# Attention scores and row maxima as float32r products in 64 rows, two side by side, and dense products cut into row halves

## The reference, cut to what matters

```python
x = x + 0.5 * ffn(layernorm(x))        # r * (relu(xk @ W_k.T)**2 @ W_v.T), r = sigmoid(xr @ W_r.T)
x = x + attention(layernorm(x))        # 16 heads of 16, rotary positions, causal softmax, projection
x = x + 0.5 * ffn(layernorm(x))
# attention:
qkv = x @ W_qkv + b_qkv
att = einsum('bhqd,bhkd->bhqk', rope(q), rope(k)) / sqrt(16)
att = where(causal, att, -1e9); att = softmax(att, axis=-1)
y = einsum('bhqk,bhkd->bhqd', att, v)
```

## Time and profile before

| | us |
|---|---|
| median of 3 runs (3110.26 to 3119.8) | 3111.19 |
| the profiled execution | 3112.07 |
| its span on the core | 3110.3 |

### The profile page before, as it was taken

One profiled execution on the slowest core, in us unless ns is written; L12 is line 12 of the kernel. 1 busy time (PEld: TensorE's weight loads), 2 busy tenths in 40 slices (PEclk: granted clock), 3 DMA queues, 4 the chain that ended last, 5 costly groups with the idle time before them and its releaser, 6 DMA issues.

```text
span 3110.3 us, 56224 instructions
## 1 busy us (share of the span) xinstructions
PE 2962.3 (95%) x18245; PEld 1665.9 (54%) x18245; DVE 2475.0 (80%) x7302; ACT 2159.2 (69%) x4802; POOL 1566.6 (50%) x2190
## 2 busy tenths in 40 slices
PE   6899999999999999999999999999999999999997
PEld 4444555555555555555555555555555555555444
DVE  3888888888888888888888887888888888887872
ACT  4477777777777777777777777777767777777664
POOL 5455555555455455555555455454555555454323
PEclk9899999999999999999999999999999999999999
DMA  3443343343434352342443333343442532433421
GB/s 99 79 84 65 64 100 66 83 90 72 86 77 88 69 97 67 76 99 60 91 87 68 88 77 84 80 85 76 79 93 59 98 81 67 93 76 71 83 60 39
DMA packets 202585, 245.49 MB, mean 79 GB/s; under 512 B 68405, under 2 KB 104245, under 8 KB 202293
## 3 DMA queue, kind: packets, MB, share of 16 engines
q1 hardware_dynamic: 202293, 241.90, 37.5%
HBM read 53.48 MB, written 51.38 MB: 34 GB/s over the span
## 4 chain that ended last, share of the span: by engine, by line
PE 66%; DVE 12%; ACT 8%; POOL 6%; issue 6%; DMA 1%; SPq 1%; POOLq 0%; DVEq 0%; ACTq 0%
PE ps_y L735 14%; PE ps_s L704 12%; PE ps_m L714 11%; PE ps_d L794 7%; PE ps_d L788 6%; PE ps_d L791 5%; PE ps_d L800 5%; ACT pt_sb L830 4%; DVE ps_m L943 3%; PE ps_d L781 3%; PE ps_d L742 2%; DVE mx_sb L946 2%; PE ps_d L804 2%; POOL pt_sb L1075 2%; DVE dif_sb L974 2%
## 5 line engine op out<-in xcount | busy, mean ns | idle before, releaser
L830 ACT ACTIVATE pt_sb<-ps_s 128x512 f32<-128x512 f32 (+1 forms) x3039 | 1451.6, 495 | 816.9 <-PE ps_s L704 806.7
L943 DVE CUSTOM_DVE_ANT_0 ps_m<-ps_m,mask_sb 128x128 f32<-128x128 f32 (+3 forms) x2048 | 990.3, 498 | 370.7 <-PE ps_m L714 355.9
L704 PE MATMUL ps_s<-qr_sb,kr_sb 99*128 99x512 bf16 (+1 forms) x3039 | 994.5, 329 | 50.4 <-ACT pt_sb L830 39.3
L714 PE MATMUL ps_m<-kr_sb,qr_sb 96*128 96x512 bf16 (+3 forms) x3072 | 1000.1, 329 | 37.9 <-DVE mx_sb L943 27.7
L946 DVE TENSOR_REDUCE mx_sb<-ps_m 128x1 f32<-128x512 f32 x1024 | 697.9, 682 | 105.7 <-PE ps_m L714 97.3
L1075 POOL TENSOR_SCALAR_AFFINE_SELECT pt_sb<-pt_sb 128x512 f32<-128x512 f32 x512 | 331.4, 647 | 833.8 <-ACT pt_sb L830 833.3
L735 PE MATMUL ps_y<-pt_sb,v_sb 128*32 128x512 f32 (+3 forms) x6144 | 589.9, 494 | 3.6 <-POOL pt_sb L1075 2.7
L704 PEld LDWEIGHTS ps_s<-qr_sb,kr_sb 99*128 99x128 bf16 x3039 | 291.8, 96 | 510.0 <-issue 229.7
L714 PEld LDWEIGHTS ps_m<-kr_sb,qr_sb 96*128 96x128 bf16 x3072 | 302.0, 98 | 319.2 <-DVE mx_sb L943 71.1
L800 PE MATMUL ps_d<-axn_sb,wqk_sb 128*128 128x256 f32 x1024 | 305.3, 396 | 3.9 <-ACT axn_sb L872 3.9
L735 PEld LDWEIGHTS ps_y<-pt_sb,v_sb 128*32 128x32 f32 x6144 | 154.6, 109 | 285.9 <-issue 258.3
(11 more groups left out here) (96 smaller groups left out, 3465.5 us busy)
## 6 DMA issues: line engine op xcount, KB each, us to landing
kr_sb<-part_sb SPq DMA_DIRECT2D x378, 128.0 KB, 4.4
qr_sb<-part_sb SPq DMA_DIRECT2D x378, 128.0 KB, 4.7
y_way<-yt_sb SPq DMA_DIRECT2D x128, 256.0 KB, 2.7
sw_sb<-qb_sb SPq DMA_DIRECT2D x496, 64.0 KB, 2.0
x_sb<-x SPq DMA_DIRECT2D x64, 256.0 KB, 2.8
yn_sb<-y_way SPq DMA_DIRECT2D x64, 256.0 KB
den_sb<-r_way SPq DMA_DIRECT2D x64, 256.0 KB
out<-x_sb SPq DMA_DIRECT2D x64, 256.0 KB, 2.2
```

The source lines that it names most:

```text
L704: eng.matmul(score_bank(slot)[:, 0:width], kr_sb[0:KR + NP, n % RS, j, kb * P:(kb + 1) * P], qr_sb[0:KR + NP, n % RS, j, q0:q0 + width], s ...
L714: eng.matmul(ps_m[:, u % NM, 0:width], qr_sb[0:KR, n % RS, j, i * P:(i + 1) * P], kr_sb[0:KR, n % RS, j, piece * QC:piece * QC + width], s ...
L830: eng.activation(pt_sb[:, buffer, j, column:column + width], score_bank(slot)[:, 0:width], ACT.Exp, scale=SCALE).then_inc(exped, 1)
L943: eng.tensor_tensor_reduce(ps_m[:, u % NM, 0:width], ps_m[:, u % NM, 0:width], mask_sb[:, m0:m0 + width], 1.0, -3e38, ALU.add, ALU.max, be ...
```

## The change

1. q and k are split into two float32r parts (`r_hi`, `r_low`) instead of three bfloat16 ones. Three products of parts (48 rows) give a score, and two rows more (50) the maximum. `r_mid` and `r_rest` go.
2. Heads 0 and 2 have their rows in partitions 0 to 49, heads 1 and 3 in 64 to 113. Score j of a slot and the maximum of head `j ^ 1` therefore stand in different row halves of the array. `BESIDE` puts a maximum of the same width beside each score. Products narrower than 256 columns are computed 256 wide (`max(CH, width)`).
3. Every dense product in the steady part is cut into two halves of 64 rows, "lane" 0 and 1, that add into the same bank. Lane 1 of a product starts when its lane 0 is complete (`half_made`), beside lane 0 of the next product. Transposes are cut in the same way, lane 0 ahead of the slot's score, lane 1 behind its maximum. `ps_d` has three banks, `ps_m` two. Outside the steady part products stay whole.
4. The causal mask of the maxima is a further product into the last 128 columns (`later_sb`, `pairs_sb`, bfloat16, 64 rows), so that DVE's part is a plain reduction in all cases.
5. The rotation works in the places of the parts; `r_b0` (ACT) now waits for the rows of the batch before, where `r_hi` did. Row copies are `rows0` to `rows2` with four DMAs each, of 128 KB as before. `m_fin` has three instructions, where it had five.

```diff
-TERMS_Q = (0, 0, 0, 1, 1, 2)
-TERMS_K = (0, 1, 2, 0, 1, 0)
+TERMS_Q = (0, 0, 1)
+TERMS_K = (0, 1, 0)
-NP = 3
+NP = 2
+HALF = P // 2
-NS, NM, ND = 2, 3, 2
+NS, NM, ND = 2, 2, 3
-MAX_ORDER = [i for k in range(TT // 2) for i in (TT - 1 - k, k)]
-LEAD = 13
+BESIDE = [(3, 0), (2, 0), (1, 0), (0, 0), (4, 0), (5, 0), (6, 0), (7, 0), (7, 1), (6, 1), (5, 1), (4, 1)]
+LEAD = 17
+NU = GSLOTS
+UNITS = [(*BESIDE[m // G][:1], m % G ^ 1, BESIDE[m // G][1]) for m in ((u - LEAD) % GSLOTS for u in range(NU))]
...
-                    s("ACT", "r_mid", i, 0.53, t, ("r_rest", i, 3))
-                    s("POOL", "r_low", i, 1.2, t, ("r_mid", i, 2))
+                    s("ACT", "r_hi", i, 0.53, t, ("r_add", i, 3))
+                    s("POOL", "r_low", i, 1.2, t, ("r_hi", i, 2))
...
+        done = 0
+        for lane in (1, 0):
+            if self.lanes[lane]:
+                key, u = self.lanes[lane]
+                units = self.steps[key][1]
+                if u < units:
+                    mine.append((*key, u, lane))
+                self.lanes[lane] = key, u + 1
+                if lane == 1 and u + 1 == units:
+                    self.lanes[1] = None
...
+                if lane == 0 and u + 1 >= units and self.lanes[1] is None:
+                    self.lanes = [None, (key, 0)]
...
-        qr_sb = sb("qr_sb", [P, RS, G, T], BF16)
-        kr_sb = sb("kr_sb", [P, RS, G, T], BF16)
+        qr_sb = sb("qr_sb", [P, RS, G // 2, T], F32R)
+        kr_sb = sb("kr_sb", [P, RS, G // 2, T], F32R)
...
-                eng.matmul(score_bank(slot)[:, 0:width], kr_sb[0:KR + NP, n % RS, j, kb * P:(kb + 1) * P],
-                           qr_sb[0:KR + NP, n % RS, j, q0:q0 + width], start=True, stop=True).then_inc(scored, 1)
+                rows, more = slice(HALF * (j % 2), HALF * (j % 2) + KR + NP), max(0, CH - width)
+                eng.matmul(score_bank(slot)[:, 0:width + more], kr_sb[rows, n % RS, j // 2, kb * P:(kb + 1) * P],
+                           qr_sb[rows, n % RS, j // 2, q0 - more:q0 + width], start=True, stop=True).then_inc(scored, 1)
...
                 pe.wait_ge(max_taken, u - NM + 1)
...
+                rows, wide = slice(HALF * (j % 2), HALF * (j % 2) + KR), max(CH, width)
+                product = eng.matmul(ps_m[:, u % NM, 0:wide], qr_sb[rows, n % RS, j // 2, i * P:(i + 1) * P],
+                                     kr_sb[rows, n % RS, j // 2, piece * QC:piece * QC + wide], start=True, stop=not diagonal)
+                if diagonal:
+                    half = slice(HALF * (j % 2), HALF * (j % 2) + HALF)
+                    pe.wait_ge(masks_in, 32)
+                    product = eng.matmul(ps_m[:, u % NM, width - P:width], later_sb[half, :], pairs_sb[half, :], start=False, stop=True)
...
+                if u == 0 and lane == 1:
+                    pe.wait_ge(half_made[d], plan.split[name, i])
...
+                if u == units - 1:
+                    mm.then_inc(half_made[d] if lane == 0 else made[d], 1)
...
-                if diagonal:
-                    eng.tensor_tensor_reduce(ps_m[:, u % NM, 0:width], ps_m[:, u % NM, 0:width], mask_sb[:, m0:m0 + width],
-                                             1.0, -3e38, ALU.add, ALU.max, best).then_inc(max_taken, 1)
-                else:
-                    eng.tensor_reduce(best, ps_m[:, u % NM, 0:width], mybir.AxisListType.X, ALU.max).then_inc(max_taken, 1)
+                eng.tensor_reduce(mx_sb[:, n % 2, piece, m:m + 1], ps_m[:, u % NM, 0:width], mybir.AxisListType.X,
+                                  ALU.max).then_inc(max_taken, 1)
```

More of the change, by code:

```diff
@@ L10 @@
 BF16 = mybir.dt.bfloat16
+F32R = mybir.dt.float32r
 ALU = mybir.AluOpType
@@ L254, in apart, with free_banks, hold, divide @@
         return math.ceil(lag * 0.5) if slot < HALF_MAX else lag
+    def free_banks(self, slot):
+        return [d for d in range(ND) if self.held[d] is None or self.slots.get(self.held[d], slot) < slot - 1]
+    def hold(self, key, d):
+        self.held[d] = self.READER[key[0]], key[1]
+        self.bank[key], self.nth[key] = d, self.uses[d]
+        self.uses[d] += 1
+    def divide(self, key):
+        d = self.bank[key]
+        self.splits[d] += 1
+        self.split[key] = self.splits[d]
@@ new lines, in pick @@
+    def pick(self, e, chains, slot, xt):
+        best = None
+        for name, line in chains.get(e, {}).items():
+            if not line or name[1:] == "_T":
+                continue
+            _, cost, rank, early, after = self.steps[name, line[-1]]
+            if early > slot or not self.ready(slot, after):
+                continue
+            if name[2:] == "x0" and xt is not None and self.slots.get(self.T_OF(xt), slot) >= slot:
+                continue
+            if e == "PE" and not self.can_make(name, line[-1], slot):
+                continue
+            if best is None or (rank, line[-1]) < best[0]:
+                best = (rank, line[-1]), name, line
+        return best and (best[1], best[2].pop())
@@ L325, in place @@
-                    key = name, line.pop()
-                    if name[2:] == "x0":
+                    if e == "PE":
+                        cost, done = self.place_pe(chains, slot, mine)
+                        if not cost:
+                            break
+                        credit[e] -= cost
+                        todo -= done
+                        continue
+                    key = self.pick(e, chains, slot, xt)
+                    if key is None:
+                        break
@@ L753, in dense @@
+                start, stop = u == 0 and not lane, False
                 if name == "f_T":
                     pe.wait_ge(f_xt, CT * (i + 1))
-                    transposes(ps, xt_sb).then_inc(made[d], 1)
-                    return
-                if name == "a_T":
+                    mm, units = transposes(ps, xt_sb, k), 1
+                elif name == "a_T":
                     pe.wait_ge(a_xt, CT * (i + 1))
-                    transposes(ps, xt_sb).then_inc(made[d], 1)
-                    return
@@ L810, in _ @@
                     pv([n_ticks - NTK + k for k in BURSTS[-1]])
+                turns = plan.at["PE"].get(slot, ())
+                for name, i, u, lane in turns:
+                    if name[1:] == "_T" and lane == 0:
+                        dense(name, i, u, lane)
                 if slot in SCORE_AT:
@@ L814, in _ @@
                     maximum(u)
-                for name, i, u in plan.at["PE"].get(slot, ()):
-                    dense(name, i, u)
+                for name, i, u, lane in turns:
+                    if name[1:] != "_T" or lane != 0:
+                        dense(name, i, u, lane)
                 if slot in PV_SLOT:
```

426 lines of the change are left out of this document (198 added, 228 removed).

## The result

| | before | after |
|---|---|---|
| median of 4 runs | 3113.94 us | **3424.11 us** |
| lowest to highest | 3110.26 to 3119.8 | 3415.62 to 3431.03 |
| profiled execution | 3112.07 | 3415.62 |
| a group in the steady part, 700 to 2700 us | 46.85 | 50.58 |
| first four, last four groups | 210, 152 | 266, 186 |

The ratio is 1.099, 95% interval [1.0955, 1.1031]: 10% slower, where 2.6% faster was forecast and 3240 was the upper end of the range. Of some 300 us, 205 fall in groups 5 to 60 (2819 us against 2614; groups are counted from the first score, and their times are differences between starts of scores), 90 in the four groups at either end.

The account below looks back on a forecast made before the run. PE, busy 95% of the span, was taken as the bound; per group 40.9 + 2.35 + 2.0 + 0.4 = 45.65 us, 1.2 under 46.85, so -77 us over 64 groups: 3034 us, range 2880 to 3240.

Parts of the forecast that it names:

- PE's own work and other waits: On PE, per group of 48 slots: 40.9 us of work after the change plus 2.35 us of remaining waits.
- ring of the maxima: PE waiting for DVE's reductions with ps_m at two banks instead of three: +2.0 us a group, between 0 and 3.3.
- ring of the scores: Two score banks, with less slack for exponentials as PE's slot gets shorter: +0.4 us a group, between 0 and 0.8.
- the one on the clock: In the steady part the granted clock is 1.00, so nothing is to be had there; no term in the sum.
- over 90%: Sign of the rings taking all: DVE over 90% busy, with PE's wait for it the largest.
- the rings take it all: Rival at the score and maxima banks: 3.3 us given back and growing PE stalls, 47.3 a group, 3110 to 3140; chance 0.20.
- -3.6: PE's own work in one group of 48 slots falls from 44.5 to 40.9 us, 3.6 less.
- score and maximum together: Sign of being right, on PE: score and maximum start within 0.02 us of each other.
- 0.65 to 0.7 in wide slots: Sign of being right, on PE: a wide slot with dense work takes 0.65 to 0.7 us where nothing waits.
- PE's wait for DVE over 100 us: Sign of being right: PE's wait for DVE at the maxima goes from 28 us to over 100.
- the group: Sign of being right: a group in the steady part takes 45 to 46 us.
- halves not independent: Rival on PE: row halves keep strict pass order, 4.05 us more a group, 3370; chance 0.23, shared with loads sharing one path.

Follow-up runs that it names:

- e4: The changed kernel with VectorE's reductions over the maxima reading only the first 32 columns: 3219.87 us, ratio 1.034 to the kernel before.
- e6: The changed kernel with 32-column reductions of the maxima and, from the third group on, 32-column exponentials: 3045.96 us, ratio 0.978 to the kernel before.
- e3: The kernel before with two banks for the maxima instead of three, nothing else changed: 3276.97 us, ratio 1.052.
- m2: A products-only kernel repeating the kernel's patterns with and without waits for a VectorE copy: clock 0.54 for a lone dense product in one half with a wait.
- m3: A products-only kernel without waits, slots in halves or whole rows, with and without masks and bursts: a burst costs 1.63 us in halves, 1.53 in whole rows.
- e11: The changed kernel with score and maximum products made twice in the first and last batches (last: only slots with under two dense passes): 3428.24 us, ratio 1.101.

## Why the prediction was wrong

The sum said 45.65 a group; 50.58 was measured. By its own steps, from e4 and e6, with 0.37 to 0.5 us for each us at half clock:

| step | predicted | measured | how |
|---|---|---|---|
| PE's own work and other waits | 40.9 + 2.35 = 43.25 | 44.5 to 44.6 | e6's 44.97 less its clock |
| ring of the maxima | +2.0 (0 to 3.3) | +2.6 | after less e4 (2.77), less 0.1 to 0.2 of clock |
| ring of the scores | +0.4 (0 to 0.8) | +1.1 to 1.6 | e4 less e6 (2.84), less 1.3 to 1.7 of clock |
| clock | 0, not in the sum | +1.8 to 2.4 | 188 of the 2000 us at half clock |
| sum | 45.65 | 50.6 | |

**The step that failed first is the one on the clock**: "The granted clock is 1.00, so nothing is to be had there." That was read as a fact of the kernel, and it was a property of a queue that seldom waits: a bank less loses it in whole rows (e3), and after loses more of it, until both readers are out of the way (e6). That cost 1.8 to 2.4, the two rings' errors together 1.3 to 1.8 and PE's own work 1.3. Each of the three is as large as the 1.2 that I had forecast as the gain. The clock alone does not explain the result: without its part a group would still have taken 48.2 to 48.8, more than the 46.85 before. The Trainium skill (TensorE: Matmul & The Clock Gate, A second HAM failure mode: psum-queue depth-cycling) describes a kernel whose clock swings because TensorE pauses briefly and often while it cycles through PSUM banks; the trace after agrees in so far as its clock falls where PE has just paused (0.32 and 0.34 us in the rows above), and m2 adds that pauses alone need not do it. By that rule taking a bank away, which makes PE pause more often, was a rival with a price of its own. I had read the page for its order of matmuls only.

**The rings** were the right mechanism, mis-sized. +2.0 was measured as 2.6, inside its bounds, +0.4 as 1.1 or more, outside them. DVE was at 69%, not "over 90%" as I wanted it for a rival: a ring of two waits for an engine that has a third of its time free, since DVE's other work comes between two reductions. The rival "the rings take it all" had the right sign and less than a tenth of the size, 3110 to 3140, because it priced no clock, took 43.25 for all else and stopped both halves for nothing.

**PE's own work**: -3.6 became -2.3 at most, since e6 also has shorter other waits. The side by side slots are nearly as I computed (0.67 against 0.65); short by some 1.3 are terms at the joints. m3's patterns give 0.1 for each of seven bursts, 0.066 for each of 32 masks ((1.45 - 1.32) / 2 by the starts of two slots) where I had 0.055, and 0.66 for a wide slot where I had 0.65: together 0.7 + 0.3 + 0.4 a group, an estimate. How much of it occurs in the kernel was not measured.

**The ends** (90 us more in eight groups): the sum was for a steady group and was taken times 64, these eight included. They had 176 us at half clock against 20, worth 58 to 78 us. Whether the clock or waits for first loads lengthen them stays open; e11 could not tell.

Of the signs that I named: score and maximum together, yes; 0.65 to 0.7 in wide slots, yes; PE's wait for DVE over 100 us, yes with the load's row, 71.5 in the product's; the group, no. And the rival with the nearest number, halves not independent, was wrong in its mechanism.

## What to carry to other kernels

Ask of every change that makes TensorE's work shorter between waits, or uses part of its rows: what holds the clock up afterwards? Two queues of work in one engine's order share each wait; splitting the array does not split the queue, so a ring needs more slack after such a change, not less. And before a bank is moved from one ring to another, run the old kernel without that bank: e3, one changed digit, would have shown half of this result (163 of 310 us).

## What was not expected of the hardware

- Row halves are nearly free of each other: 1.92 times for float32r, 0.109 a dense pass against 0.217, and a later product of one half can start ahead of an earlier one of the other (1705.02 and 1705.13).
- A change between 64-row and 128-row products costs about 0.2 us each way (1.05 against 0.66 a pair).
- The same waits leave the clock at 1.00 with dense products in both halves and take it to 0.54 with one in one half alone.
- A burst of products with v, over all 128 rows, costs about 0.1 us more behind products in halves than behind whole ones (1.63 against 1.53).
- After a wait that stops its load, a product starts with its load, not behind it (1703.30 both), and its first record is 0.1 longer than one that was loaded ahead (0.49 against 0.38).
